# Attention with mixed heads, one core: the output product of eight tiles in two runs of 128 matmuls, and other slots for the row work

## What is computed

```python
q, k, v = split(x @ Wqkv.T + bqkv);  q, k = apply_rope(q), apply_rope(k)
logits = einsum('bhij,gh->bgij', einsum('bhid,bhjd->bhij', q, k) * SCALE, Wpre)
attn   = einsum('bhij,gh->bgij', softmax(logits, -1), Wpost)
x = layernorm(x + (einsum('bhij,bhjd->bhid', attn, v) reshaped) @ Wout.T + bout)
xn = layernorm(x) * gamma + beta;  l = einsum('bnd,des->bnes', unit(xn) * scale, unit(mu))
slot_in = einsum('bnd,bnes->besd', xn, softmax(l, over e))
out = einsum('besd,bnes->bnd', gelu(slot_in @ w1 + b1) @ w2 + b2, softmax(l, over e and s))
x = layernorm(x + out)
```

## Time and profile before

| what | value |
|---|---|
| median of the runs | 8678.64 us |
| the profiled execution, its own time | 8680.39 us |
| its span, from the first to the last instruction | 8678.4 us |
| mean granted TensorE clock | 0.985 |
| TensorE busy (matmul) | 8319.2 us, 96% |
| VectorE busy | 7725.0 us, 89% |
| ScalarE busy | 7258.7 us, 84% |
| GpSimd busy | 6656.0 us, 77% |

### The profile page before, as it was taken

The page is one execution under the profiler, slowest core; times in us unless marked ns, Lnnn a source line. Parts: engine busy times, 40 slices in busy tenths (PEclk is TensorE's granted clock), DMA queues, the critical chain, the costliest instruction groups (busy, mean ns, idle before and its releaser), DMA issues.

```text
span 8678.4 us, 399747 instructions
## 1 busy us (share of the span) xinstructions
PE 8319.2 (96%) x158060; PEld 4653.3 (54%) x158060; DVE 7725.0 (89%) x11213; ACT 7258.7 (84%) x13696; POOL 6656.0 (77%) x14053
## 2 busy tenths in 40 slices
PE   8999999998999999999889999999989999999997
PEld 4555555555555555555545555555554555555554
DVE  7999999997899999999789999999978999999996
ACT  6888888886688898888668888888857988888895
POOL 7787878875788787878478888787847878788883
PEclk9999999998999999999899999999989999999998
DMA  0000000002000000000200000000020000000002
GB/s 32 6 8 9 8 8 9 9 7 77 18 6 8 9 8 8 9 9 8 76 18 6 8 9 8 8 8 9 8 76 18 6 8 9 9 8 8 9 8 80
DMA packets 98674, 141.23 MB, mean 16 GB/s; under 512 B 7840, under 2 KB 88352, under 8 KB 94496
## 3 DMA queue, kind: packets, MB, share of 16 engines
q1 hardware_dynamic: 96800, 115.48, 4.0%
HBM read 73.51 MB, written 39.85 MB: 13 GB/s over the span
## 4 chain that ended last, share of the span: by engine, by line
PE 74%; DVE 10%; issue 9%; POOL 3%; ACT 3%; DVEq 1%; POOLq 0%; ACTq 0%
PE psS L1185 48%; PE psP L1205 16%; PE psO L1220 6%; DVE big L847 3%; DVE pl L873 2%; DVE top L838 2%; PE psM L1231 1%; ACT big L676 1%; PE psS L1322 1%; POOL pl L524 1%; PE psS L1351 1%; POOL rl L569 1%; PE psM L1246 1%; PE psS L1157 0%; ACT ew L697 0%
## 5 line engine op out<-in xcount | busy, mean ns | idle before, releaser
L847 DVE SCALAR_TENSOR_TENSOR big<-psP,big 128x512 f16<-128x512 f32 x4096 | 2622.2, 681 | 393.7 <-ACT big L676 368.5
L676 ACT ACTIVATE big<-psP 128x512 f16<-128x512 f32 x4096 | 2199.1, 588 | 719.5 <-PE psP L1205 719.2
L838 DVE TENSOR_REDUCE top<-psS 128x1 f32<-128x1024 f32 x2048 | 2488.1, 1215 | 215.0 <-PE psS L1185 214.8
L1185 PE MATMUL psS<-KH,AH 128*128 128x512 f16 x8192 | 2465.6, 383 | 64.3 <-POOL AL L465 41.7
L1185 PE MATMUL psS<-KH,AL 128*128 128x512 f16 x8192 | 2442.2, 380 | 0.0
L1185 PE MATMUL psS<-KL,AH 128*128 128x512 f16 x8192 | 2440.7, 380 | 0.0
L657 ACT ACTIVATE pr<-psS,nb 128x1024 f32<-128x1024 f32 x2048 | 2282.0, 1114 | 66.5
L686 ACT ACTIVATE ph<-pr 128x1024 f16<-128x1024 f32 x2048 | 2165.4, 1057 | 64.8
L873 DVE TENSOR_TENSOR pl<-pr,ph 128x1024 f16<-128x1024 f32 (+1 forms) x2048 | 2173.9, 1061 | 0.0
L1205 PEld LDWEIGHTS psP<-rh,ph 64*128 64x128 f16 x32768 | 1433.8, 95 | 938.3 <-DVE big L847 556.0
L1205 PE MATMUL psP<-rh,ph 64*128 64x64 f16 x32768 | 1681.8, 192 | 141.2 <-DVE big L847 133.2
(11 more groups left out here) (136 smaller groups left out, 7374.8 us busy)
## 6 DMA issues: line engine op xcount, KB each, us to landing
ph<-in_xT SPq DMA_DIRECT2D x16, 512.0 KB, 7.8
xr<-in_x SPq DMA_DIRECT2D x64, 128.0 KB, 2.2
Q<-in_w SPq DMA_DIRECT2D x8, 1024.0 KB, 7.4
out<-V SPq DMA_DIRECT2D x16, 512.0 KB, 3.9
d_x<-x SPq DMA_DIRECT2D x60, 128.0 KB, 2.0
d_xn<-xn SPq DMA_DIRECT2D x60, 128.0 KB, 2.8
d_lg<-lg SPq DMA_DIRECT2D x60, 128.0 KB, 2.2
d_ct<-cT SPq DMA_DIRECT2D x60, 128.0 KB, 1.7
```

The source lines that it names most:

```text
L676: a.activation(PT[:, hf * JH:(hf + 1) * JH, :, 0, i0:i0 + HQ], psP[:, ih, :].rearrange("p (j g i) -> p j g i", j=JH, g=H), ACT.Copy, scale ...
L838: v.tensor_reduce(top[:, t % 2, h:h + 1], psS[:, 2 * h:2 * h + 2, :].rearrange("p c n -> p (c n)"), X, ALU.max).then_inc(s_mx, 1)
L847: v.scalar_tensor_tensor(out=PT[:, js, :, 1, i0:i0 + HQ], in0=psP[:, ih, :].rearrange("p (j g i) -> p j g i", j=JH, g=H), scalar=MDROP, in ...
L1185: mm = pe.matmul(psS[:, c, :], A_[:, k8, k, :], K_[:, k, c * CW:(c + 1) * CW], start=n == 0, stop=n == 5)
```

## The change

1. TensorE: the pieces of `output` stand in pairs, pieces 0 and 1 behind the second quarter of the scores and ahead of the first turn, pieces 2 and 3 behind the fourth quarter and ahead of the second turn.
2. VectorE: `out_copy` becomes two instructions of half the size, the first behind the first two `mixed_low` of slots 3 and 11 and the second behind the last two. The semaphore `s_oc` counts two for each output, and the waits on it follow.
3. VectorE: `stats` goes to place 0 beside `residual`; `aggr` and `variances` to place 1; `halve1` and `seed1` to place 2; `centre` to the slot of `norm1` (slot 2, and slot 11 of the last iteration). `esum` stands in place 2, ahead of `combine`.
4. ScalarE: `weigh` goes from the slot's end to behind `highs` of the first half.
5. The tables: `y` goes from slot 3 to 4, the turning of xn from 4 to 5, the expert logits from 5 to 6; `weigh` from 11 to 10, `combine` from 12 to 10 and the turning of the combine weights from 13 to 11. The last iteration moves likewise.

```diff
-LATER = dict(norm=2, root2=(3, 4), turn_u=4, logits=5, keep=10, weigh=11, combine=12, turn_c=13)
+LATER = dict(norm=2, root2=(3, 4), turn_u=5, logits=6, keep=10, weigh=10, combine=10, turn_c=11)
...
-                v.tensor_reduce(ot[:, :, half * GI:(half + 1) * GI],
-                                psO[:, :].rearrange("p (q s i) -> p q i s", q=GQ, s=2), X,
-                                ALU.add).then_inc(s_oc, 1)
+                qs = slice(part * GQ // 2, (part + 1) * GQ // 2)
+                ins = v.tensor_reduce(ot[:, qs, half * GI:(half + 1) * GI],
+                                      psO[:, qs.start * P:qs.stop * P].rearrange("p (q s i) -> p q i s", s=2, i=GI),
+                                      X, ALU.add)
+                ins.then_inc(s_oc, 1)
...
                     if live:
                         scores(T, t, 0, first and t < 1)
-                    pieces(0)
                     if live:
                         scores(T, t, 1, first and t < 1)
-                    pieces(1)
+                    pieces(0, 1)
                     if two:
                         turn(T - 2, t_2, 0, fresh)
```

More of the change, by code:

```diff
@@ L68 @@
 NEWTON = 3
-FIRST = dict(bias=1, y=3, residual=10, root1=(11, 4))
-LATER = dict(norm=2, root2=(3, 4), turn_u=4, logits=5, keep=10, weigh=11, combine=12, turn_c=13)
-LATER_END = dict(norm=2, root2=(3, 2), turn_u=5, logits=6, keep=7, weigh=7, combine=8, turn_c=8)
-WHOLE = dict(bias=1, y=3, residual=4, root1=(6, 2), norm=10, root2=(11, 2), turn_u=12, logits=13, keep=14,
-             weigh=14, combine=15, turn_c=15)
+FIRST = dict(bias=1, y=4, residual=10, root1=(11, 4))
+LATER = dict(norm=2, root2=(3, 4), turn_u=5, logits=6, keep=10, weigh=10, combine=10, turn_c=11)
+LATER_END = dict(norm=2, root2=(3, 2), turn_u=6, logits=7, keep=8, weigh=8, combine=8, turn_c=9)
+WHOLE = dict(bias=1, y=4, residual=5, root1=(6, 2), norm=11, root2=(12, 2), turn_u=13, logits=14, keep=15,
+             weigh=15, combine=15, turn_c=15)
 def in_work(it):
@@ L722, in slot @@
                         highs(T, t, 0, early)
+                    for r, at in in_work(it):
+                        if t == at.get("weigh"):
+                            weigh(r)
                     mixed(2)
@@ L989, in combine, with copied @@
                     v.tensor_scalar(ew[:, :], ew[:, :], er[:, 0:1], None, ALU.mult).then_inc(s_C, 1)
+                def copied(it, t, first, part):
+                    if t % TG == 3 and not (first and t < TG) and it < NIT:
+                        out_copy((b * NIT + it) * 2 + t // TG - 1, (t // TG + 1) % 2, b * NIT + it - (1 if t < TG else 0),
+                                 part)
                 def rows(it, t, place):
@@ L1007, in rows @@
                             if t == at.get("residual"):
-                                stats(r)
-                            if t == at.get("combine"):
-                                esum(r)
+                                aggr(r)
+                                variances(r)
                         elif place == 2:
@@ L1016, in rows @@
                                 column(r)
+                            if t == at.get("combine"):
+                                esum(r)
+                                combine(r)
                             if t == at.get("residual"):
[L1018 to L1021, removed]
+                                halve1(r)
+                                seed1(r)
                         elif place == 3:
@@ L1046, in slot @@
                         mixed_low(T - 2, t_2, 1)
+                    copied(it, t, first, 0)
                     rows(it, t, 1)
@@ L1055, in slot @@
                         mixed_low(T - 2, t_2, 3)
+                    copied(it, t, first, 1)
                     if live:
@@ L1064, in _ @@
                 slot(NIT, 1, False, False)
-                out_copy((b + 1) * (NIT * 2) - 1, 1, b * NIT + NIT - 1)
+                for part in range(2):
+                    out_copy((b + 1) * (NIT * 2) - 1, 1, b * NIT + NIT - 1, part)
                 for step in (residual, stats, aggr, variances, halve1, seed1, centre, norm1, norm2, squares, bound,
```

24 lines of the change are left out of this document (9 added, 15 removed).

## The result

| what | before | after |
|---|---|---|
| median of four runs each, same chip | 8678.70 us (8676.37 to 8679.10) | 8617.72 us (8610.72 to 8621.60) |
| the profiled execution | 8680.39 us | 8610.72 us |
| its span | 8678.4 us | 8608.8 us |
| mean granted clock of TensorE | 0.985 | 0.985 |

A forecast was written before the change was run, and what follows sets the result against it. TensorE, busy 96%, was taken as the bound, its time being matmul pace plus interruptions. From 8680.4 us, -60 (switches), -94 (VectorE's order) and +88 (late packets) gave 8614 profiled, 8612 us as median, range 8535 to 8690.

The forecast's parts named there:

- Switches, -60: TensorE's output slots: pairing pieces drops one switch to output and back per half slot, 0.24 us each, -60 us.
- VectorE's order, -94: Turns waiting for mixed_low in slots 3 and 11 to 13: moving copy and row steps saves 94 us.
- its first margin: Second turn of slot 11: mixed_low done at 1049.9, 0.4 us ahead of the turn due at 1050.34.
- the 0.3 that I kept: Turns' waits for mixed_low in iterations 1 to 14: 0.3 us of the 2.0 per iteration remain.
- where the copy and the centring stand: VectorE: the argument, against the rival of staying waits, that the turns' waits sit at these two steps.
- Packets, +88: TensorE's runs of 128 output matmuls plus turn: instruction packets come late at 27 edges a batch, +88 us.
- The first rival (8512): Instruction fetch in the longer runs: packets are asked for earlier and never late, 8512 us; chance 0.13.
- the second (8739): Instruction fetch in the longer runs: each of 27 edges a batch costs 2.1 us, 8739 us; chance 0.14.
- place 22 or later: Output runs whose first edge lies there, 13 a batch: transfer 0.8 after the edge plus 2.55, 1.45 us late.
- The early places: Output runs with the first edge in places 0 to 21, 11 a batch: transfer starts ahead, 0.35 us late.
- Waits that stay (8676): Turns' waits for VectorE: margins are used up, only 30 of the 94 us come, 8676 us; chance 0.16.
- The sum: Whole kernel: the terms -60, -94 and +88 us together, giving a median of 8612 us, 0.8% faster.

The follow-up runs named there:

- experiment 10: Changed kernel with experiment 5's added instructions, first number 90, so each first run of 128 meets an edge at its 8th matmul: 8543.57 us, ratio 0.9845.
- experiment 11: Kernel of experiment 1 (single pieces) with the added instructions of experiment 5, 123 again as the first number: 8604.02 us, ratio 0.9914.
- experiment 3: Kernel before with only the output copy in two parts behind mixed_low, and y with what follows it a slot later: 8664.6 us, ratio 0.9987.
- experiment 4: Changed kernel with the output copy whole again and ahead of the first mixed_low: 8642.52 us, ratio 0.9966.
- experiment 8: Kernel before with only the row steps from stats to centre moved: 8637.08 us, ratio 0.9951.
- experiment 9: Kernel before with only weigh, esum, combine and the turning of the combine weights moved: 8652.02 us, ratio 0.9971.
- experiment 5: Changed kernel with small added waits inside TensorE's scores, so that no run of output and turn holds two packet edges: 8543.07 us, ratio 0.9843.
- experiment 6: As experiment 5 with 88 instructions fewer ahead of the first output, so each first run and its turn hold two edges: 8699.81 us, ratio 1.0024.
- experiment 1: Changed kernel with the four output pieces single again, each behind its own quarter of the scores: 8595.28 us, ratio 0.9910.
- experiment 2: Kernel before with only the pairing of the output pieces: 8704.81 us, ratio 1.0037.
- experiment 12: Experiment 5 with first number 118 in place of 123 and the last rows' norm in slot 10 of iteration 15: 8529.37 us, ratio 0.9828.

## Why the prediction was right, step by step

*Switches, -60.* Right: -55 by the trace. The 60 us between experiments 10 and 11 holds 16 of late scores in experiment 11 besides, and is no second measure of it.

*VectorE's order, -94.* Right in sum (-88), and in its first margin: 0.4 us to spare at the second turn of slot 11, measured 1042.43 less 1042.02. Turns still wait where I had put the smallest margins, 0.08, 0.11 and 0.03 us of an iteration in slots 12 to 14, and 0.26 in slot 4: 0.48 for the 0.3 that I kept. Iteration 15 was no worse than before (4.5 us for 4.7), where I had 5.5. But one argument behind the term was weak: I took the waits to sit "where the copy and the centring stand". Experiments 3 and 4 refute that for the copy. With its 0.58 us out of the way the kernel gains 10 us alone and 10 to 32 beside the row moves, because what stands ahead of a wait and what stands behind it are one backlog that drains only in slots with slack. The centring (42 us, experiment 8) and the combine weights (27, experiment 9) carry the term. That I walked the clock through four slots, and not one, is why the sum came out.

*Packets, +88.* The mechanism is shown by experiments 5 and 6: they differ in 88 added instructions ahead of the first output, which shift the numbering, and the gaps come and go with it. The Trainium skill's page "Runtime: NRT & Kernel Launch", section "Instruction fetch mechanics", holds that issue is too slow for the fetch to be seen; in runs of this pace the trace disagrees, by 131.6 us in experiment 6. The first rival (8512) and the second (8739) are both out.

The size was a little high: +78. Where the first edge lies at place 22 or later, all 13 outputs of a batch were late in all four batches, by 0.90 to 1.76 us, mean 1.23, for my 1.45. (The transfers there start 0.47 to 1.34 us behind the edge, median 0.7 for my 0.8, and the code runs 2.2 to 2.7 us after that, for my 2.55.) The three with the second edge just behind the turn were 0.7 late, for 0.85. The early places came out right by luck. There are 11, as I had, and their mean is 0.33, for my 0.35; but it is made of two kinds. In the five that are the first run of their slot it was 0.05 in the mean, which experiment 10 bears out for all 31; in the six that are second runs it was 0 to 1.14, 0.56 in the mean. The instruction queue's records go with this: ahead of the first runs the transfer starts between 1.77 us ahead of the edge and 0.03 behind it, 1.4 ahead in the median; in the second runs between 0.45 ahead and 0.68 behind. So its start hangs on more than the place of the edge in its run. A likely cause, argued only, is what lies in the passage before, which takes 7.0 to 8.2 us ahead of a first run and 4.56 ahead of a second, where it holds another run of output.

One reading in the working is loose: an edge has its second in the turn if it lies in the first 48 pairs of the run, not 54. The three at pairs 53 and 54 have it in the scores behind; the counts of 24 and 3 have this right.

*Waits that stay (8676).* Not seen: the turns wait 0.48 us an iteration, a quarter of what it was.

*The sum.* That it comes within 1 us in the slots (-65 for -66) is in part luck: two terms gave 5 and 6 us less than I had put, and the third cost 10 less.

*What I did not see* is that the pairing, which I booked as a gain of 60 and a loss of 88, should have been read as one edit with the sum +28. The two terms stood in my own working. Experiments 1 and 2 give +16 to +22 and +30.

## What to carry to other kernels

Book an edit's gain and its side effect as one term before adding it to the others: here a net loss of 16 to 30 us stood behind a gain of 55. When an in-order engine waits at several places in a row, its waits are one backlog; taking work from the first place moves the wait, so walk the clock on until there is slack. When an engine runs a few hundred small instructions at full pace, look in the trace for gaps with no releaser, and number the instructions. If the gaps fall a fixed distance apart, shift the code with cheap instructions. Place them between slow instructions: right behind a fast run, 4 to 8 of them cost 0.07 to 0.54 us each time (experiment 11).

## What the runs showed of the hardware

- The place of the code alone moved the time by 157 us, 1.8% (experiments 5 and 6). TensorE's instructions come in packets of 256: counted from a batch's first scores, all gaps of over 0.3 us inside output and turns lie on one place of 256, within 2, in the kernels before and after and in experiments 2 and 6, and with 4 x 1699 instructions more the queue's packets rise from 1270 to 1298. In a run of 128 output matmuls and the 48 of a turn, one edge cost next to nothing (0.5 us in all in the 248 runs of experiment 5); two cost 1.24 us in 124 of 124 with the first edge at the 36th matmul, and nothing in 124 of 124 with it at the 8th (experiment 10). With the first edge at the 36th the packet's transfer starts 0.47 to 1.24 us behind that edge, at the 8th 0.60 to 1.77 ahead of it.
- 1699 instructions more in each batch, inside the scores, cost nothing that shows: all that scores start late behind scores, summed over the slots, is 38.9 us in experiment 10 and 38.7 in experiment 1, which has none of them. From the first to the last scores of a batch it is 1997.5 us in the changed kernel, 1977.1 in experiment 5, 1975.8 in experiment 10 and 1973.9 in experiment 12, on the mean of the four. From there to the next batch it is 146.1 us in the changed kernel and 151.0 in experiment 10, where that code has new numbers; but it is 149.1 in experiment 1 with the old ones, so part of this is spread. That stretch was not tuned.
- A packet's lateness is not fixed by the program: at one output of the changed kernel, with the first edge at the 29th matmul, it was 1.74, 1.76, 1.19 and 1.19 us in the four batches.
